# A cross-attention and feed-forward kernel: TensorE's operands placed at other SBUF addresses, and M's halves regrouped by even and odd heads

## What is computed

```
x = x + attention(layernorm(x), ctx)         # q = h Wq, k = ctx Wk, v = ctx Wv; 8 heads of 64; softmax(q k^T / 8) v; then Wo, + bo
x = x + 0.5 * (silu(ln(x) @ w1 + b1) @ w2 + b2)   # ln with gamma and beta; w1 (256 x 1024) and w2 (1024 x 256)
                                                  # are (q - 128) * scale, with one scale per 128 rows and column
```

## Time and profile before

| | us |
|---|---|
| median of 3 runs (lowest to highest) | 193.17 (192.78 to 193.65) |
| the profiled execution | 193.64 |
| its span, first to last instruction | 191.9 |
| PE busy / PEld busy in the span | 184.8 (96%) / 181.4 (95%) |
| DVE, ACT, POOL busy | 124.4 (65%), 121.7 (63%), 116.0 (60%) |
| granted TensorE clock | 1.000 |

### The profile page before, as it was taken

How to read it: one execution, slowest core, us unless ns; L and a number is a source line. 1 busy time by engine, 2 the same in 40 slices (tenths; PEclk the granted TensorE clock), 3 DMA queues, 4 the chain that set the end, 5 groups by cost and what they waited for, 6 DMA issues and landing times.

```text
span 191.9 us, 3879 instructions
## 1 busy us (share of the span) xinstructions
PE 184.8 (96%) x1502; PEld 181.4 (95%) x1502; DVE 124.4 (65%) x262; ACT 121.7 (63%) x227; POOL 116.0 (60%) x159
## 2 busy tenths in 40 slices
PE   6999989989899999999999999999999999999994
PEld 6989879789899999999999999999999999999894
DVE  0097997999969464964496558846693668165441
ACT  3157790499918981898378935895289717952580
POOL 5031997459983977098708962597449663768020
PEclk9999999999999999999999999999999999999999
DMA  6995793000000100010001000100001000100101
GB/s 168 318 406 148 219 388 110 2 0 4 2 0 0 58 0 0 3 55 0 3 0 55 3 0 0 33 29 0 0 19 40 0 3 0 55 3 0 55 3 55
DMA packets 9480, 10.72 MB, mean 56 GB/s; under 512 B 2268, under 2 KB 8183, under 8 KB 9335
## 3 DMA queue, kind: packets, MB, share of 16 engines
q1 hardware_dynamic: 8837, 9.70, 15.2%
q10 hardware_dynamic: 626, 0.79, 1.5%
HBM read 8.38 MB, written 2.10 MB: 55 GB/s over the span
## 4 chain that ended last, share of the span: by engine, by line
PE 85%; DVE 12%; issue 1%; ACT 0%; POOL 0%; POOLq 0%
PE T L801 22%; PE H L789 20%; PE S L756 13%; PE T L777 13%; PE S L763 4%; PE S L710 3%; PE S L688 2%; DVE w_lo L587 2%; PE T L740 2%; DVE hT_lo L569 1%; DVE q_sb L581 1%; PE H L740 1%; PE T L729 1%; PE T L695 1%; DVE smax L520 1%
## 5 line engine op out<-in xcount | busy, mean ns | idle before, releaser
L286 POOL TENSOR_TENSOR y_lo<-y,y_hi 128x512 fp32r<-128x512 f32 x28 | 37.5, 1363 | 3.0 <-ACT y_hi L397 2.9
L254 POOL TENSOR_TENSOR probs<-probs,rsum 128x616 f32<-128x616 f32 x16 | 19.1, 1218 | 32.3 <-DVE rsum L539 32.3
L789 PE MATMUL H<-hT_hi,w_hi 128*128 128x256 f32 x128 | 37.2, 291 | 1.2 <-issue 0.8
L801 PE MATMUL T<-w_hi,y_hi 128*128 128x256 f32 x128 | 36.8, 288 | 0.5 <-DVE w_lo L587 0.5
L801 PE MATMUL T<-w_lo,y_hi 128*128 128x256 f32 x128 | 35.7, 279 | 0.0
L801 PE MATMUL T<-w_hi,y_lo 128*128 128x256 f32 x128 | 35.7, 279 | 0.0
L789 PE MATMUL H<-hT_hi,w_lo 128*128 128x256 f32 x128 | 35.7, 279 | 0.0
L789 PE MATMUL H<-hT_lo,w_hi 128*128 128x256 f32 x128 | 35.6, 278 | 0.0
L393 ACT ACTIVATE y<-H,vec 128x256 f32<-128x256 f32 x64 | 26.6, 468 | 8.3 <-PE H L789 8.3
L366 ACT ACTIVATE probs<-probs,rstd 128x616 f32<-128x616 f32 x16 | 12.9, 807 | 27.4 <-DVE probs L527 27.4
L789 PEld LDWEIGHTS H<-hT_hi,w_hi 128*128 128x128 f32 x128 | 24.1, 188 | 1.8 <-issue 1.2
(11 more groups left out here) (119 smaller groups left out, 461.3 us busy)
## 6 DMA issues: line engine op xcount, KB each, us to landing
q_sb<-in_L_ffn_fc_q SPq DMA_DIRECT2D x2, 1024.0 KB, 8.1
out_x<-x_sb SPq DMA_DIRECT2D x16, 128.0 KB, 1.8
x_sb<-in_x SPq DMA_DIRECT2D x7, 256.0 KB, 8.2
s_sb<-in_L_ffn_fc_scales SPq DMA_DIRECT2D x2, 512.0 KB, 11.4
s_sb<-in_L_ffn_fc_scales SPq DMA_DIRECT2D x1, 1024.0 KB, 7.8
wq_sb<-in_L_xattn_Wq SPq DMA_DIRECT2D x1, 512.0 KB, 5.7
wo_sb<-in_L_xattn_Wo SPq DMA_DIRECT2D x1, 512.0 KB, 8.2
wk_sb<-in_L_xattn_Wk ACTq DMA_DIRECT2D x1, 384.0 KB, 4.3
```

Of the source, the lines that this page charges most:

```text
L254: nc.gpsimd.tensor_tensor(p, p, rsum[:, j, :].unsqueeze(2).to_broadcast([P, HEADS, J]), ALU.mult).then_inc(norm_done, 1)
L286: nc.gpsimd.tensor_tensor(y_lo[:, two, :], y[:, two, :], f32(y_hi[:, two, :]), ALU.subtract).then_inc(y_lo_done, 1)
L789: ins = mm(r[:, q * W:(q + 1) * W], wt[:, c, m * P:(m + 1) * P], ht[:, c, :], start=i == 0, stop=i == len(steps) - 1)
L801: ins = mm(o, yt[:, m, j * P:(j + 1) * P], wt[:, m, :], start=m == 0 and i == 0, stop=m == M - 1 and i == 2)
```

## The change

Three things change, and no instruction is added, removed or moved on any engine.

1. **Addresses.** The order of the allocations is new, with two paddings of 64 bytes (`skew`, `skew_end`) and one behind the small tensors. The starts modulo 128, for the tensors that TensorE reads:

| stream | stationary before, after | moving before, after | stationary minus moving, modulo 128, before, after |
|---|---|---|---|
| S, L756 | xT 32, 0 | m 64, 16, 96, 48, 0, 80, 32, 112 (by half, 128 rows of x and batch), all 64 | eight values, 64 |
| AO, L777 | pT 96, 0 | vw 64, 64 | 32, 64 |
| F1, L789 | w1 64, 0 | hT 0, 64 | 64, 64 |
| F2, L801 | y 0, 0 | w2 64, 64 | 64, 64 |
| PT, L763 | probs 32, 0 | ident 64, 0 | 96, 0 |
| XT and HT, L710 | x_sb 0 and hn 0, the same | ident 64, 0 | 64, 0 |
| projections K and V, L695 | wk, wv 0, the same | ctxT 0, the same | 0, 0 |

   Slices in these tensors step by multiples of 512 bytes, but for M, whose halves are 1232 bytes long before.

2. **M's halves.** A half is now padded to 320 columns (1280 bytes, ten times 128), of which 308 are read. The first half holds the even heads and the second the odd ones, so that `m_hi_part` and `m_lo_part` write 308 columns in one piece, where they wrote four pieces of 77.

3. **Head order.** `subtract_maxima` puts the heads back in their natural order: it writes `probs` in eight pieces of 77 columns, where it wrote 616 in one piece. The maxima `smax` are in the order of S, and everything behind `probs` is as before.

```diff
+LINE = 128
+SKEW = 64
+GRAIN = 32
@@
+    HALF_COLS = -(-HALF * 4 // LINE) * LINE // 4
@@
+        used = 0
+        def small(name, shape):
+            nonlocal used
+            used += -(-math.prod(shape[1:]) * 4 // GRAIN) * GRAIN
+            return sb(name, shape)
         x_sb = sb("x_sb", [P, NT, D])
...
         w1_hi, w1_lo = sb("w1_hi", [P, C, F], F32R), sb("w1_lo", [P, C, F], F32R)
+        xT_hi, xT_lo = sb("xT_hi", [P, C, W], F32R), sb("xT_lo", [P, C, W], F32R)
+        pT_hi, pT_lo = sb("pT_hi", [P, UT, JC, P], F32R), sb("pT_lo", [P, UT, JC, P], F32R)
+        hT = sb("hT", [P, C, W])
+        hn = sb("hn", [P, UT, D])
+        y = sb("y", [P, M, W])
+        probs = sb("probs", [P, UT, JC * P])
+        ident = sb("ident", [P, P])
...
+        sb("skew", [P, SKEW // 4])
         w2_hi, w2_lo = sb("w2_hi", [P, M, D], F32R), sb("w2_lo", [P, M, D], F32R)
-        m_hi, m_lo = sb("m_hi", [P, B, C, 2, HALF], F32R), sb("m_lo", [P, B, C, 2, HALF], F32R)
+        m_hi, m_lo = sb("m_hi", [P, B, C, 2, HALF_COLS], F32R), sb("m_lo", [P, B, C, 2, HALF_COLS], F32R)
         vw_hi, vw_lo = sb("vw_hi", [P, B * JC, D], F32R), sb("vw_lo", [P, B * JC, D], F32R)
...
         hT_hi, hT_lo = sb("hT_hi", [P, C, W], F32R), sb("hT_lo", [P, C, W], F32R)
+        sb("skew_end", [P, (LINE - SKEW) // 4])
+        vec = small("vec", [P, 2 * C + M])
...
+        sb("rest_of_line", [P, (LINE - used % LINE) // 4])
@@
         def m_heads(m, b, n):
-            return m[:, b, n // 2, :, :].rearrange("p h (k e j) -> p (h k) e j", k=K // 2, e=2)[:, :, n % 2, :]
+            return m[:, b, n // 2, n % 2, 0:HALF]
@@
-                    nc.scalar.activation(m_heads(m_hi, b, n), r[:, 0:HALF].rearrange("p (k j) -> p k j", k=K), ACT.Copy,
+                    nc.scalar.activation(m_heads(m_hi, b, n), r[:, 0:HALF], ACT.Copy,
@@
-                    nc.vector.scalar_tensor_tensor(m_heads(m_lo, b, n), ps[bank][:, 0:HALF].rearrange("p (k j) -> p k j", k=K), DH ** -0.5 / D,
+                    nc.vector.scalar_tensor_tensor(m_heads(m_lo, b, n), ps[bank][:, 0:HALF], DH ** -0.5 / D,
@@
-                    nc.vector.tensor_tensor(probs[:, j, 0:HJ].rearrange("p (n h j) -> p n h j", n=2, j=J), s,
+                    nc.vector.tensor_tensor(probs[:, j, 0:HJ].rearrange("p (h n j) -> p n h j", n=2, j=J), s,
@@
-                            ins = mm(o, xt[:, c, j * P:(j + 1) * P], m[:, b, c, h, :], start=n == 0, stop=n == len(steps) - 1)
+                            ins = mm(o, xt[:, c, j * P:(j + 1) * P], m[:, b, c, h, 0:HALF], start=n == 0, stop=n == len(steps) - 1)
```

More of the change, by code:

```diff
@@ L1 @@
+import math
 from contextlib import ExitStack
@@ L80, in sem @@
             return stack.enter_context(nc.semaphore(name))
-        x_sb = sb("x_sb", [P, NT, D])
[L83 to L87, removed]
+        used = 0
[3 more added lines that the diff above has]
+            return sb(name, shape)
+        x_sb = sb("x_sb", [P, NT, D])
         q1_sb = sb("q1_sb", [P, C, F], I32)
@@ L93, in build_program @@
         w1_hi, w1_lo = sb("w1_hi", [P, C, F], F32R), sb("w1_lo", [P, C, F], F32R)
+        xT_hi, xT_lo = sb("xT_hi", [P, C, W], F32R), sb("xT_lo", [P, C, W], F32R)
[5 more added lines that the diff above has]
+        ident = sb("ident", [P, P])
+        bo_sb = sb("bo_sb", [1, D])
+        bo_hi, bo_lo = sb("bo_hi", [1, D], F32R), sb("bo_lo", [1, D], F32R)
@@ L94, in build_program @@
+        b2_half = sb("b2_half", [P, D])
+        sb("skew", [P, SKEW // 4])
         w2_hi, w2_lo = sb("w2_hi", [P, M, D], F32R), sb("w2_lo", [P, M, D], F32R)
-        m_hi, m_lo = sb("m_hi", [P, B, C, 2, HALF], F32R), sb("m_lo", [P, B, C, 2, HALF], F32R)
+        m_hi, m_lo = sb("m_hi", [P, B, C, 2, HALF_COLS], F32R), sb("m_lo", [P, B, C, 2, HALF_COLS], F32R)
         vw_hi, vw_lo = sb("vw_hi", [P, B * JC, D], F32R), sb("vw_lo", [P, B * JC, D], F32R)
-        ident = sb("ident", [P, P])
-        neg_half = sb("neg_half", [P, NT])
@@ L100, in build_program @@
[L100 to L113, removed]
-        hT_hi, hT_lo = sb("hT_hi", [P, C, W], F32R), sb("hT_lo", [P, C, W], F32R)
-        y = sb("y", [P, M, W])
+        hT_hi, hT_lo = sb("hT_hi", [P, C, W], F32R), sb("hT_lo", [P, C, W], F32R)
@@ new lines, in build_program @@
+        sb("skew_end", [P, (LINE - SKEW) // 4])
+        vec = small("vec", [P, 2 * C + M])
+        gamma_sb, beta_sb, b1_sb = vec[:, 0:C], vec[:, C:2 * C], vec[:, 2 * C:2 * C + M]
+        neg_half = small("neg_half", [P, NT])
+        table_probe = small("table_probe", [P, 1])
+        bn1, mv1 = small("bn1", [P, NT, 6]), small("mv1", [P, NT, 2])
+        veps1, rstd1 = small("veps1", [P, NT]), small("rstd1", [P, NT])
+        smax, ssum, rsum = small("smax", [P, UT, HEADS]), small("ssum", [P, UT, HEADS]), small("rsum", [P, UT, HEADS])
@@ L119, in build_program @@
+        bn2, mv2 = small("bn2", [P, 2, UT, 6]), small("mv2", [P, 2, UT, 2])
+        vars2, rstd2 = small("vars2", [P, 2, 2, UT]), small("rstd2", [P, 2, 2, UT])
+        neg_rstd2, res_scale, res_shift = small("neg_rstd2", [P, 2, UT]), small("res_scale", [P, 2, UT]), small("res_shift", [P, 2, UT])
+        sb("rest_of_line", [P, (LINE - used % LINE) // 4])
         early = ExitStack()
```

## The result

The changed kernel takes 193.66 us (median of 20 runs, 193.09 to 194.34), the kernel before 193.08 (20 runs, 192.57 to 193.65). The ratio is 1.0025 with a 95% interval of 1.0015 to 1.0036: slower by a quarter of a per cent, where I had forecast 0.7% faster.

The account below looks back on a forecast made before the run. The prediction took TensorE's stream pace to bound the kernel from 50 us on; AO's 0.84 and S's 0.36 us sum to 1.20, giving 192.0 on the median 193.17, stated as 191.9; range 190.4 to 194.0, the forecast's own 191.2 to 192.6.

Parts of the forecast that it names:

- What bounds the kernel: From 50 us to the end the kernel runs at the pace of TensorE's streams; one matmul shape has three paces.
- What the paces go with: Weight load and matmul disturb each other reading SBUF; operand distance modulo 128 sets how much, 64 best of those seen.
- F1 and F2 at nothing: F1 and F2 stay at distance 64, costed at zero; ends 1.1 us saved and 1.4 us lost.
- the rival that spreads the slow pace: F1 takes F2's slow habit, F1 and F2 lose 1.4 us; 194.0 us; decides once over half of fast F1 turns slow; chance 0.12.
- AO: AO's distance goes from 32 to 64: 210 matmuls save 4.0 ns each, 0.84 us, ends 0.42 and 1.37.
- S: All S distances become 64: 108 matmuls that count save 3.3 ns each, 0.36 us, ends 0.14 and 0.63.
- the wait ahead of F1: PE waits for split_h in pairs 2 to 6; gains of S(a,1) and F2(a-2,1) only lengthen it, by 0.1 us or so.
- Transposes, DVE and ACT: Moved ident and the strided write cost zero; upper ends 0.6 us lost on transposes, 0.4 us on DVE.
- Nothing moves: Rival: the paces come of something the change leaves alone; time 193.2 us; chance 0.18.
- All fast: Rival: AO at 113.5 ns, S at 135.5, F1 and F2 fast, 3.1 us saved, 190.1 us; chance 0.12.

Follow-up runs that it names:

- f_d64: Changed kernel with moving operands 192 bytes further than stationary in place of 64, all four streams at 64 modulo 256; 191.49 us, ratio 0.9914 to the kernel before.
- f_dist0: Changed kernel without its two paddings of 64 bytes, both operands at 0 modulo 128; 194.73 us, ratio 1.0088 to the kernel before.
- p_ring: Measuring stand, TensorE streams alone: sixteen distances modulo 256, 256 and 308 columns; with 256, distance 0 has 119.6 to 120.0 ns, 192 has 117.8.
- b_ao192: Kernel before with only pT moved by 32 bytes, so AO stands at 192 modulo 256; 191.93 us, ratio 0.9934.
- b_ao64: Kernel before with only pT moved by 160 bytes, so AO stands at 64 modulo 256; 192.89 us, ratio 0.9983.
- a_f1_64: Changed kernel with hT_hi and hT_lo 128 bytes later, F1 back at 64 modulo 256; 192.92 us, ratio 0.9986 to the kernel before.
- f_d64_s224: f_d64 with xT moved by 160 bytes, so S stands at 224 modulo 256; 191.33 us, ratio 0.9898 to the kernel before.
- f_mirror: Changed kernel with sides swapped in all large TensorE streams, stationary at 64 and moving at 0; 193.09 us, ratio 1.0002 to the kernel before.
- a_lead6: Changed kernel with the last of each tile's five probability transposes done twice; one execution, 195.97 us.
- p_entry: Measuring stand: bursts at 64 and 192 modulo 256 behind 1 to 8 float32 matmuls, other engines quiet or busy; 192 never falls from its slow pace.
- p_distance: Measuring stand, TensorE streams alone: 48 bursts at eight distances modulo 128, either operand at 0; at 64 one burst of three is fast in the first half.

## Why the prediction was wrong

*What bounds the kernel* was right. From F2(0,0) to the end the chain takes 139.13 us before, 139.69 in the changed kernel and 137.60 in f_d64, which is 0.56 more and 1.53 less; the medians differ by 0.58 and 1.65. The two paces, 113.3 and 117.8 ns, recur in all full kernels but f_dist0. One reading was off: the 116 ns of F1's 1.39 / 12 is not a mean of two paces. The single steps of those pieces come down to 113 to 115 ns after two to five steps, and the rest of the 116 is their entry behind the transposes.

*What the paces go with* is the step that failed. I took the distance modulo 128 and so put F1 (64) and F2 (192) in one class, though one of them is mostly fast and the other mostly slow: the difference stood in the earlier trace rows and I gave it to chance. The runs put 256 at least in its place, and p_ring's 144 shows that the distance modulo 256 is not all of it. Of the streams behind transposes, F1 at 64 modulo 256 falls into the fast pace in all its pieces of 12 in seven traces (the two of the kernel before, b_ao192, b_ao64, a_f1_64, f_d64, f_d64_s224), at 192 in 5 of 36 (changed kernel, f_mirror, a_lead6).

*F1 and F2 at nothing* is the term that this mis-sized: 0 forecast, 0.95 us lost on the chain. F1's 0.57 come of its distance, as a_f1_64 shows. F2's 0.38 do not, for its distance stayed at 192, and their cause is open. The loss lies within the end that I gave the term, 1.4, and the rival that spreads the slow pace, at 194.0, had the effect right: of the 264 F1 matmuls that stood in fast pieces 72 are left, so the point from which it decides was passed. Its reason was wrong: it is not the side that stands at 0, as f_mirror shows for F1. That 193.66 lies inside the range of 190.4 to 194.0 is owed to this rival alone; the forecast's own range ended at 192.6.

*AO* was right in kind, and its size came out at the low end: 1.9 ns in place of 4.0 (117.8 ns, where I took 116), 0.41 us in place of 0.84.

*S* was wrong: 0 in place of 0.36. The scatter went, and the mean stayed at 141.5 ns, since the distance it got, 192, has 141.6 with 308 columns; 64 is worse still, and of the distances that a full kernel had, 0 and 224 are best (p_ring, f_dist0, f_d64_s224). That the wait ahead of F1 takes what S(a,1) and F2(a-2,1) gain was right, and f_d64 shows it with F2's gain.

*Transposes, DVE and ACT* at nothing were right: PT is at 0.55 us for five, XT at 0.44 for four, L712 at 1.05 for eight, L544 at 799 ns.

*Nothing moves* fell: b_ao192, b_ao64 and f_d64 change nothing but addresses in SBUF, and AO's pace changes by up to 6.4 ns. (TensorE's outputs lie in PSUM, not in SBUF, and no edit of a full kernel moves them there.) The Trainium skill, "TensorE: Matmul & The Clock Gate", Part 2 (what happens when you issue a matmul), has the two operands on independent read ports, so that loading weights takes no read bandwidth from the running matmul. The traces don't agree with what the prediction drew from it, that no distance matters.

*All fast* is what f_d64 almost is. It has 1.65 us of the 3.1, since S is slower there, some F1 pieces of 24 stay slow, and part of the gain goes into waits. Its argument that a fast burst hands its phase on doesn't hold in general: in a_f1_64 the last F1 stream is fast and F2 behind it slow throughout.

Open remains what picks AO's pace. At 192 it is slow in the changed kernel and a_f1_64 and fast in b_ao192; at 64 it is slow in b_ao64 and fast in f_d64. Two candidates can be struck out for 192: by the layout the distance is the same even modulo 1024 (448) in a_f1_64 and b_ao192, and F1's piece ahead is fast in both. (For 64 the first of them stays: 576 in b_ao64, 320 in f_d64.) What still differs is where each operand stands above 256 bytes and the addresses of the F1 stream ahead; none of the runs tells them apart.

## What to carry to other kernels

Where weight loads and matmuls run side by side without a gap, compare the step from start to start of equal streams: a few nanoseconds between them can be a matter of operand addresses alone, worth 1% here, and padding of a few hundred bytes tries it out. Take the distance modulo at least 256 and don't trust it alone, measure each width by itself, and test the arrangement in the whole kernel, for a stand gave the possible paces and not the one that a stream would take. Before regrouping everything to one distance, ask which stream is already good, and keep its distance as it is.

## What the runs showed of the hardware

At the 2.4 GHz level (granted clock 1.00 over the bursts) a float32r matmul of 256 columns with its weight load takes 113.3 or 117.8 ns from start to start at distances of 64 and 192. In the stands 64 has both paces and 192 only the slower one; in full kernels both distances have both. The patterns are locked (113, 113, 114), last to the end of a burst and are the same with the other engines quiet or busy (p_entry). Over all distances tried the pace goes from 113.3 to 120.3 ns, and with 308 columns from 139.8 to 146.7 (p_distance, p_ring). Which of two paces a burst takes at 64 depended on the number of float32 matmuls ahead of it. Float32 transposes showed no trace of a distance: 110 ns for 128 columns at 0, 64 and 96 modulo 128 (before, after).
